# Flamingo block, layer 0: the transposes of W_qr and W_kr in one group and one bank

## The reference

```python
q_hk = (hidden_q @ Wq.T).reshape(Bv, Sv, H, K)
q_big = jnp.einsum('bshk,hkq->bshq', q_hk, w_kc_q)
q_big = _apply_rope(q_big, sin_q[None, :, None, :], cos_q[None, :, None, :])   # layer 0 only
q_r = jnp.einsum('bshq,hqr->bhsr', q_big, W_qr)
k_r = jnp.einsum('bld,hdr->bhlr', kv_r, W_kr)
scores = jnp.einsum('bhsr,bhlr->bhsl', q_r, k_r)
attn = jax.nn.softmax(scores, axis=-1)
ctx_c = jnp.einsum('bhsl,bld->bhsd', attn, kv_r)
ctx_lat = jnp.einsum('bhsd,hkd->bhsk', ctx_c, w_kc_kv)
return ctx @ Wo.T
```

## Time and profile before

| | |
|---|---|
| median of 3 runs | 1016.87 us (1015.41 to 1019.77) |
| profiled execution | 1016.85 us |
| its span, first to last instruction | 1014.8 us |
| mean granted TensorE clock | 0.990 |
| TensorE busy | 950.2 us, 94% |
| VectorE busy | 662.4 us, 65% |
| ScalarE busy | 528.3 us, 52% |
| GpSimd busy | 518.4 us, 51% |

### The profile page before, as it was taken

One profiled execution on the slowest core, in us unless ns is written; L12 is line 12 of the kernel. 1 busy time (PEld: TensorE's weight loads), 2 busy tenths in 40 slices (PEclk: granted clock), 3 DMA queues, 4 the chain that ended last, 5 costly groups with the idle time before them and its releaser, 6 DMA issues. The chain is left out here.

```text
span 1014.8 us, 19581 instructions
## 1 busy us (share of the span) xinstructions
PE 950.2 (94%) x6132; PEld 566.5 (56%) x6141; DVE 662.4 (65%) x1180; ACT 528.3 (52%) x1238; POOL 518.4 (51%) x652
## 2 busy tenths in 40 slices
PE   3779999999999999999989899999999999989998
PEld 1335565556555556644445567767777664445443
DVE  5887878787878777588677656666667654313012
ACT  2355666666566656400477377776777762116300
POOL 4687767777877776305333366666566651200000
PEclk9999999999999999999999899999999999999999
DMA  9232313232413222251010210222102006013001
GB/s 247 77 87 70 108 50 115 53 112 59 124 42 115 65 80 82 79 199 67 13 72 32 102 49 28 73 72 72 45 28 72 1 1 238 1 30 147 1 31 41
DMA packets 30344, 75.56 MB, mean 74 GB/s; under 512 B 4967, under 2 KB 11239, under 8 KB 28126
## 3 DMA queue, kind: packets, MB, share of 16 engines
q1 hardware_dynamic: 24706, 66.31, 20.8%
q10 hardware_dynamic: 5596, 8.70, 3.1%
HBM read 63.98 MB, written 3.68 MB: 67 GB/s over the span
## 5 line engine op out<-in xcount | busy, mean ns | idle before, releaser
L1279 POOL TENSOR_SCALAR scratch<-scratch,rinv 112x375 f32<-112x375 f32 x256 | 149.0, 595 | 139.5 <-DVE rinv L1119 139.5
L982 ACT ACTIVATE scratch<-ps,mxn 112x375 f32<-112x375 f32 x256 | 144.0, 570 | 36.5 <-DVE mxn L1114 35.0
L524 PE MATMUL ps<-arena 128*128 128x512 f16 x672 | 149.3, 379 | 1.2 <-PEq L685 1.2
L1114 DVE TENSOR_REDUCE mxn<-ps 112x2 f32<-112x750 f32 x128 | 119.7, 935 | 41.9 <-PE ps L759 41.4
L1260 POOL TENSOR_TENSOR scratch<-scratch 128x448 f32<-128x448 f32 x64 | 110.1, 1729 | 36.0 <-DVE scratch L1137 22.8
L813 PE MATMUL ps<-xnT,scratch 128*128 128x448 f16 x576 | 120.8, 356 | 4.6 <-DVE scratch L1193 3.5
L1271 POOL TENSOR_TENSOR scratch<-scratch 128x375 f16<-128x375 f32 x128 | 119.4, 933 | 10.9
L800 PE MATMUL ps<-scratch,kvn_hi 125*128 125x224 f16 x768 | 119.9, 260 | 3.2 <-DVE scratch L1159 2.3
L785 PEld LDWEIGHTS ps<-ident,scratch 112*125 112x125 f32 x768 | 101.1, 188 | 26.9 <-issue 19.9
L1137 DVE TENSOR_TENSOR scratch<-ps,ropeq 128x448 f32<-128x448 f32 x192 | 110.0, 615 | 3.4 <-PE ps L813 3.1
L1182 DVE TENSOR_TENSOR scratch<-ps,scratch 125x672 f16<-125x672 f32 x128 | 108.7, 849 | 5.4 <-ACT scratch L992 5.4
(11 more groups left out here) (166 smaller groups left out, 1413.2 us busy)
## 6 DMA issues: line engine op xcount, KB each, us to landing
scratch<-in_wq SPq DMA_DIRECT2D x16, 512.0 KB, 4.4
scratch<-in_wo SPq DMA_DIRECT2D x16, 512.0 KB, 3.6
wabs<-in_w ACTq DMA_DIRECT2D x32, 256.0 KB, 3.0
scratch<-in_w SPq DMA_DIRECT2D x8, 1024.0 KB, 4.8
scratch<-in_W SPq DMA_DIRECT2D x8, 1024.0 KB, 6.0
scratch<-scratch SPq DMA_DIRECT2D x64, 112.0 KB, 2.3
scratch<-in_kcq SPq DMA_DIRECT2D x8, 512.0 KB, 3.5
scratch<-in_qr SPq DMA_DIRECT2D x32, 128.0 KB, 3.5
```

Source lines behind the costliest of these rows:

```text
L524: last = nc.tensor.matmul(ps[:, bank, :], a[:, h, t * P:(t + 1) * P], c[:, h, :], start=(h == 0 and i == 0), stop=(h == H - 1 and i == 2))
L982: last = nc.scalar.activation(prob[0:S, s % 2, hh, :], scores_ps[0:S, hh, 0:L], ACT.Exp, bias=mxn[0:S, s % 2, hh:hh + 1], accum_out=rsum[0 ...
L1114: nc.vector.tensor_reduce(mxn[0:S, s % 2, :], scores_ps[0:S, :, 0:L], AX_X, ALU.max, negate=True).then_inc(max_done, 1)
L1279: last = nc.gpsimd.tensor_scalar(prob[0:S, s % 2, hh, :], prob[0:S, s % 2, hh, :], rinv[0:S, s % 2, hh:hh + 1], P_SCALE, ALU.mult, ALU.mult)
```

## The change

In layer 0 the group R is gone from the three tables. G makes four transposes into its one bank: the queries' weights in columns 0 to 383, the keys' weights in columns 384 to 511. G is now a split kind in layer 0: ScalarE makes `wkr_hi` from the last 128 columns, and VectorE, when that is done, copies the first 384 columns to `wqr` and makes `wkr_lo`. Waits for R become waits for G. Layer 1 keeps G and R apart.

```diff
--- before.py
+++ after.py
@@ -73,7 +73,7 @@
     [TURN, SCORES, *ropes(3, 0, 1), ("S", 2), ("K", 4), ("U", 0)],
     [TURN, SCORES, ("S", 3), ("A", 0), ("C", 1), ("K", 5)],
     [TURN, SCORES, *ropes(0, 2, 0), ("S", 4), ("K", 6), ("A", 1)],
-    [TURN, SCORES, *ropes(0, 1), ("S", 5), ("K", 7), ("G", 0), ("R", 0), *ropes(1, 2)],
+    [TURN, SCORES, *ropes(0, 1), ("S", 5), ("K", 7), ("G", 0), *ropes(1, 2)],
     [TURN, SCORES, *ropes(1, 0, 1), ("S", 6), ("K", 0), ("U", 1)],
     [TURN, SCORES, ("S", 7), ("A", 2), ("C", 0), ("K", 1)],
 ], [
@@ -93,7 +93,7 @@
     [TURN, ("S", 2), EXPS, ("K", 4), ("U", 0)],
     [TURN, ("S", 3), EXPS, ("H", 1), ("A", 0), ("C", 1), ("K", 5)],
     [TURN, EXPS, ("S", 4), ("K", 6), ("A", 1), ("V", 2)],
-    [TURN, EXPS, ("S", 5), ("K", 7), ("R", 0), ("V", 3)],
+    [TURN, EXPS, ("S", 5), ("K", 7), ("G", 0), ("V", 3)],
     [TURN, ("S", 6), EXPS, ("K", 0), ("U", 1)],
     [TURN, ("S", 7), EXPS, ("A", 2), ("C", 0), ("K", 1)],
 ], [
@@ -113,7 +113,7 @@
     [SCORES, *ropes(3, 0), TURN, *ropes(3, 1), ("S", 2), NORM, ("L", 0), ("U", 0)],
     [SCORES, TURN, ("S", 3), NORM, ("L", 1), ("A", 0), ("C", 1)],
     [SCORES, *ropes(0, 2), TURN, *ropes(0, 0), NORM, ("S", 4), ("A", 1)],
-    [SCORES, TURN, *ropes(0, 1), NORM, ("S", 5), ("G", 0), ("R", 0), *ropes(1, 2)],
+    [SCORES, TURN, *ropes(0, 1), NORM, ("S", 5), ("G", 0), *ropes(1, 2)],
     [SCORES, *ropes(1, 0), TURN, *ropes(1, 1), ("S", 6), NORM, ("U", 1)],
     [SCORES, TURN, ("S", 7), NORM, ("A", 2), ("C", 0)],
 ], [
@@ -151,7 +151,8 @@
      (7, 6): (0, 1), (7, 7): (0, 2), (8, 0): (0, 2), (8, 1): (0, 2), (8, 2): (1, 1)},
 )
 EARLY_HEADS = 2 * (PAIRS - 1)
-SPLIT_KINDS = ("A", "C", "U", "M", "Q", "R")
+
+SPLIT_KINDS = (("A", "C", "U", "G"), ("U", "M", "Q", "R"))
 
 
 def flamingo(nc, x_d, out_d, w, tab):
@@ -549,7 +550,8 @@
             mixed = order[at["A", 0]:N_THIS] if layer == 0 else []
             N_AHEAD = N_THIS - len(mixed)
             last_u = max((("U", 0), ("U", 1)), key=lambda g: (g in this, at[g]))
-            split_order = [g for g in order if g[0] in SPLIT_KINDS]
+            split_order = [g for g in order if g[0] in SPLIT_KINDS[layer]]
+            made_keys = ("G", 0) if layer == 0 else ("R", 0)
             NS = len(split_order)
             split_at = {g: i for i, g in enumerate(split_order)}
             tag = f"l{layer}"
@@ -677,8 +679,9 @@
                     half = slice(n * B // 2, (n + 1) * B // 2)
                     return (src[:, 0:HALF].rearrange("p (b n) -> p b n", b=B // 2),
                             qr_hi[:, half, 0:S], qr_lo[:, half, 0:S], c_scale)
-                if kind == "R":
-                    return src[:, 0:2 * R], wkr_hi, wkr_lo, W_SCALE
+                if kind in ("G", "R"):
+                    first_col = DCQ if kind == "G" else 0
+                    return src[:, first_col:first_col + 2 * R], wkr_hi, wkr_lo, W_SCALE
                 return src, mq_hi, mq_lo, M_SCALE
 
 
@@ -703,7 +706,7 @@
                     def weights(q, *names):
                         def free(n):
                             if n == "qr":
-                                sp.wait_ge(group_done, nth_group(q - 1, ("R", 0)))
+                                sp.wait_ge(group_done, nth_group(q - 1, made_keys))
                             elif n in ("kckv", "wo"):
                                 sp.wait_ge(group_done, nth_group(q - 1, last_u))
                             elif layer == 0:
@@ -764,7 +767,7 @@
                     def keys(p, g):
                         q, b = pair_of(p, g), g[1]
                         wait_bank(pe, p, g)
-                        pe.wait_ge(group_out, nth_group(q, ("R", 0)))
+                        pe.wait_ge(group_out, nth_group(q, made_keys))
                         if layer == 0 and (first(p) or isinstance(p, int) and p == 0 and b >= 2):
                             pe.wait_ge(kv_low, b + 1)
                         for i, (v, j) in enumerate(((wkr_hi, 0), (wkr_hi, 1), (wkr_lo, 0))):
@@ -869,7 +872,7 @@
                                                             start=(c == 0), stop=(c == QK - 1))
                         if kind == "G":
                             pe.wait_ge(raw["qr"], nth(q, 1, 0) * 32)
-                            for c in range(QK):
+                            for c in range(QK if layer == 1 else QK + 1):
                                 last = nc.tensor.transpose(out[:, c * P:(c + 1) * P],
                                                            raw_qr[:, c * P:(c + 1) * P], eye)
                         if kind == "R":
@@ -1013,7 +1016,7 @@
                             sums_high(*batch(p, g[1], 3), g[1])
                         if g[0] == "K":
                             keys_out(p, g)
-                        if g[0] not in SPLIT_KINDS:
+                        if g[0] not in SPLIT_KINDS[layer]:
                             return
                         q = pair_of(p, g)
                         act.wait_ge(group_done, nth_group(q, g))
@@ -1147,8 +1150,11 @@
                         if kind == "K":
                             return
                         q = pair_of(p, g)
-                        if kind in SPLIT_KINDS:
+                        if kind in SPLIT_KINDS[layer]:
                             dve.wait_ge(group_high, nth_split(q, g))
+                            if kind == "G":
+                                nc.vector.tensor_copy(wqr.rearrange("p c n -> p (c n)"),
+                                                      bank(p, g)[:, 0:DCQ])
                             if kind == "U":
                                 h = ds(2 * q + n, 1)
                                 nc.vector.scalar_tensor_tensor(
```

## The result

| | before | after |
|---|---|---|
| median of 20 runs each, in the comparison | 1017.4 us | 1014.45 us |
| lowest, highest | 1015.41, 1019.82 | 1012.57, 1017.96 |
| ratio, 95% interval | | 0.9968 (0.996 to 0.9976) |
| span of the profiled execution | 1014.8 us | 1010.6 us |

By the ratio the change makes the kernel 0.32% faster, 3.3 us, with an interval from 2.4 to 4.1 us (the two medians are 2.95 us apart). The forecast was 2.8 us and "no change that a measurement can tell".

What follows compares the result with a forecast made beforehand. TensorE, busy 94% of the span, was taken to bound the kernel. Savings of 2.52 us in the loop and 0.27 in the first pass, 2.8 us, took 1016.87 to 1014.1 us; range 1011.6 to 1018.

Steps and rivals of the forecast that it cites:

- The place and the gap: Layer 0's loop over head pairs: TensorE bounds; its 0.56 us wait moves from ahead of R to ahead of B(1,2).
- What the move gives: TensorE, layer 0: B(1,2) starts where R started, saving 0.36 us seven times and 0.27 in the first pass, 2.79 us.
- The bound of 0.92 us if B(1,2) did not wait: Layer 0's loop: upper bound of 0.56 + 0.36 us an iteration, 7.4 us for eight, without any wait ahead of B(1,2).
- VectorE's order: Copy waits for ScalarE's high half, at most about 0.05 us; B(1,2)'s rope starts 0.2 us earlier, U1 stays covered; cost nothing.
- the rival that gives the gain back: High half, copy and low half in a row on one bank delay ropes, U1 waits; 1016.3 to 1016.9 us, chance 0.17.
- First pass, edge, other queues: First pass gains 0.27 us; B(2,2) at the loop's edge keeps 0.97 us cover; SyncE, GpSimd and other queues cost nothing.
- The sum: Whole kernel: 2.52 us from the loop plus 0.27 from the first pass, 2.8 us, giving 1014.1 us.
- No change that can be told: Whole kernel's measured time: within about 0.5%, 5.1 us, of the kernel before; chance 0.87.
- The vanished gap: Ahead of B(1,2): it finds its bank free and the gap goes as well, 7.4 us, 1009.5 us; chance 0.06.
- Late exponentials: ScalarE's slot 5 exponentials delay the high half, VectorE's rope of B(1,2) and U1; slower, 1021 to 1024 us; chance 0.04.

Runs made afterwards that it cites:

- old banks: The changed kernel with number 27 skipped in the bank turn, so that B(1,2) takes S5's bank, not B(0,1)'s; 1016.67 us, ratio 0.9992 to the kernel before.
- the rope first: The changed kernel with VectorE roping B(0,1) ahead of the turning in slot 5; 1013.43 us, ratio 0.9966 to the kernel before.

## Why the prediction was right

*The place and the gap: right.* TensorE bounds the loop, the gap stays and moves from ahead of R to ahead of B(1,2), now 0.45 us, and G with four transposes (0.60 us) ends inside it.

*What the move gives: the size right, the cause wrong.* The step reads "What goes is R's place behind it", 0.36 us each in the loop. The rows show 0.36, and 0.38 by the iterations, but R's place is 0.11, and in the loop even that cost nothing. B(1,2) had a wait of its own. VectorE ends B(0,1)'s rope at 227.93 and S5's sums at 228.28, 0.35 us apart. Before, B(1,2) had to wait for the second, and R ran in between; with the shorter turn it waits for the first. That difference is the gain. The old banks take it away with the four transposes left in one group, and two more transposes behind the gap cost 0.03. I had worked out the bank of B(1,2) after the change and not the one before; R's row at 227.98 and 0.33 us long looked as if it filled the time. In the first pass, which has no sums, the step was right: nothing but R stood between the rope and B(1,2), and it took 0.27 us.

The number came out all the same, and not by luck: it was taken from R's start to B(1,2)'s start, and the forecast had worked out that B(1,2) takes over R's gate. It really starts 0.05 us behind the rope, as R did, and then the whole distance goes, whatever filled it. The wrong cause would have misled whoever counted on R's place by itself, as the kernel with the old banks shows.

*The bound of 0.92 us if B(1,2) did not wait: too high.* With the rope first it doesn't wait, and 0.57 us an iteration go against the kernel before (46.52 to 45.95); the rest comes back ahead of the turning and U1.

*VectorE's order: right, with the margin too small.* I put the rope of B(1,2) 0.2 us earlier. It moved by 0.35 against the rope of B(0,1) (2.43 us behind it before, 2.08 now), and starts 0.88 us behind B(1,2) as ever (0.87). The high half was ready 0.1 us ahead of VectorE. U1 (230.29) starts 0.38 us behind the end of B(1,0)'s rope (229.91), where the forecast left 0.2. So the rival that gives the gain back didn't happen. By the rule of the Trainium skill, PSUM — Partial Sum Buffer, section "PSUM bank collisions raise a hardware error", ScalarE's high half and VectorE's copy must not be in their one bank at the same time. The trace has them one after the other, till 226.01 and from 226.12, and it costs TensorE nothing; nor does it in the kernel where the same order makes VectorE idle for 0.37 us. What an overlap would do no run here shows.

*First pass, edge, other queues: right.* 0.26 us against 0.27; no new wait at the edge.

*The sum.* Seven times 0.36 to 0.38 and 0.26 make 2.8 to 2.9 us. The times say 3.3, from 2.4 to 4.1. "No change that can be told" was the likeliest outcome at a bound of 0.5%, and 0.32% lies inside it; twenty runs of each kernel tell it from nothing all the same.

*The rivals.* The vanished gap needs VectorE's rope earlier, as the forecast said, and brings 0.57 us an iteration where the forecast named 0.92. Late exponentials didn't occur. What was missing among them is what the experiments showed: that the gain in the loop comes from the bank number and not from the work taken out.

## What to carry to other kernels

A wait that the profile names is the last gate of one instruction; before counting on it, look for the gate of the next instruction behind it, in the weight loads too, and write down for each group which buffer it reuses before and after. Taking a group out of a rotation changes the buffer of everything behind it and, for the next few groups, whom they wait for; that can be worth more than the group. Work that stands in the shadow of a wait is free there, and costs in full where it is moved into the open.

## What the runs showed of the hardware

The start of the kernel is not the same from one profile to the next. Here are the twelve matmuls of A1 in the first pass, which no edit touches, in the kernel before and then with the old banks:

```profile
28.70 2.44 PE L813 MATMUL ps<-xnT,scratch 128*128 128x448 f16 x12 [0.68 <-DVE scratch L1137]
```

```profile
29.63 4.23 PE L816 MATMUL ps<-xnT,scratch 128*128 128x448 f16 x12
```

The same twelve take 2.44 us in the one and 4.23 in the other, and the granted clock is recorded as 1.00 in both. In the kernel before, the three B matmuls of a block take 0.73 us at 30.98, as they do in the loop at a clock of 1.00; with the old banks that pace shows first at 33.70. So there was slow pace without a recorded low clock at the start; why, these runs don't show.

Later the recorded clock does fall, in both, but not at the same place. In the kernel before it is 0.69 in the mean from 34 to 36 us and 0.50 of full, 1.2 GHz, from 36 to 38, behind an idle time of 2.40 us. With the old banks the idle time ahead of G is 0.82 us, and the clock stays at 1.00 there. It is 0.65 from 60 to 62 us and 0.50 from 62 to 64, behind an idle time of 1.65 us:

```profile
59.51 0.96 PE L476 MATMUL ps<-ident,arena 125*128 125x125 f32 x6 [1.65 <-DVE kvT L500]
```

From the first G to the next it took 53.24 us in the kernel before (34.10 to 87.34) and 51.79 with the old banks (35.24 to 87.03). Of these 1.45 us 0.83 lie between the starts of G and B(1,2), where the one kernel has a wait and R and the other has neither; the rest lies in the next few microseconds, where the clocks differ. So this stretch can't be compared without looking at both. What comes before it differs too: in the two profiles of the changed kernel the first G starts at 33.50 and 34.97 us and the spans are 1010.6 and 1011.8, while from the first G to the next they take 52.94 and 52.95 us. I compared iterations of the loop instead, where the clock is 1.00 and these two profiles agree within 0.02 us.
